# Fused cross-attention and expert layer: P times V for two quads of heads in one group, four buffers for P, and the output normalised ahead of a maximum

## What is computed

```python
qh = (q @ Wq + bq).reshape(B, LQ, HEADS, D_K).transpose(0, 2, 1, 3)
kh = (k @ Wk + bk).reshape(B, LKV, HEADS, D_K).transpose(0, 2, 1, 3)
vh = (v @ Wv + bv).reshape(B, LKV, HEADS, D_K).transpose(0, 2, 1, 3)
scores = jnp.einsum('bhqd,bhkd->bhqk', qh, kh) * scale
attn = jax.nn.softmax(scores, axis=-1)
out = jnp.einsum('bhqk,bhkd->bhqd', attn, vh)
concat = out.transpose(0, 2, 1, 3).reshape(B, LQ, D_MODEL)
return concat @ Wo + bo
```

## Time and profile before

| what | before |
|---|---|
| median of three runs | 1063.61 us (1063.42 to 1067.46) |
| profiled execution, its own time | 1062.17 us |
| its span | 1060.4 us |
| TensorE multiplies busy | 885.8 us, 84% |
| TensorE weight loads busy | 700.0 us, 66% |
| VectorE busy | 698.5 us, 66% |
| ScalarE busy | 616.3 us, 58% |
| GpSimd busy | 227.5 us, 21% |
| granted TensorE clock, mean | 0.928 |

### The profile page before, as it was taken

How to read it: one execution, slowest core, us unless ns; L and a number is a source line. 1 busy time by engine, 2 the same in 40 slices (tenths; PEclk the granted TensorE clock), 3 DMA queues, 4 the chain that set the end, 5 groups by cost and what they waited for, 6 DMA issues and landing times. The chain is left out here.

```text
span 1060.4 us, 23352 instructions
## 1 busy us (share of the span) xinstructions
PE 885.8 (84%) x8843; PEld 700.0 (66%) x8843; DVE 698.5 (66%) x1884; ACT 616.3 (58%) x1305; POOL 227.5 (21%) x192
## 2 busy tenths in 40 slices
PE   0763789999999999999999850039999999999995
PEld 0331357767676776777676640029999999999995
DVE  6681267787778777877878648857566576574540
ACT  1432477777777777777776531009568476485671
POOL 1343000000000000000000004042556466565313
PEclk9986699999999999999999975559999999999998
DMA  2211674565566456546644012031533524525203
GB/s 69 70 35 35 154 161 116 143 156 124 118 156 143 122 131 157 129 121 147 151 114 101 24 34 77 0 127 34 125 83 95 128 46 123 128 49 137 40 11 35
DMA packets 96209, 104.63 MB, mean 99 GB/s; under 512 B 11744, under 2 KB 92272, under 8 KB 96112
## 3 DMA queue, kind: packets, MB, share of 16 engines
q1 hardware_dynamic: 84128, 88.50, 33.5%
q0 software_dynamic: 10752, 14.69, 8.1%
q10 hardware_dynamic: 1232, 0.12, 0.1%
HBM read 39.60 MB, written 14.68 MB: 51 GB/s over the span
## 5 line engine op out<-in xcount | busy, mean ns | idle before, releaser
L405 DVE TENSOR_REDUCE a_nm<-a_pS 112x1 f32<-112x375 f32 x512 | 264.7, 543 | 122.8 <-PE a_pS L500 119.8
L350 ACT ACTIVATE a_P<-a_pT 128x448 f32<-128x448 f32 x384 | 209.2, 546 | 136.0 <-PE a_pT L494 135.3
L500 PE MATMUL a_pS<-kst,a_qst 96*112 96x375 bf16 x512 | 151.9, 336 | 3.6 <-DVE a_nm L405 3.1
L494 PE MATMUL a_pT<-a_qst,kst 98*128 98x112 bf16 x1536 | 139.3, 213 | 1.6 <-DMA a_qst<-a_mT 1.5
L494 PEld LDWEIGHTS a_pT<-a_qst,kst 98*128 98x128 bf16 x1536 | 107.4, 99 | 42.7 <-issue 8.6
L1278 PE MATMUL e_p<-w2h,e_hh 128*128 128x256 f32 x448 | 128.3, 286 | 0.0
L1278 PE MATMUL e_p<-w2h,e_hl 128*128 128x256 f32 x448 | 126.2, 282 | 0.0
L1278 PE MATMUL e_p<-w2l,e_hh 128*128 128x256 f32 x448 | 126.2, 282 | 0.0
L358 ACT ACTIVATE kp<-a_pK,bk 128x375 bf16<-128x375 f32 x192 | 109.5, 570 | 19.1 <-PE a_pK L524 12.1
L1133 POOL DMA_INDIRECT out_dram<-e_y,e_idx x56 | 88.3, 1577 | 134.0 <-ACT e_y L1162 130.3
L879 POOL MEMSET r_factors<- 128x1 f32 x15 | 0.6, 98 | 540.2 <-POOLq L236 539.9
(11 more groups left out here) (193 smaller groups left out, 1506.3 us busy)
## 6 DMA issues: line engine op xcount, KB each, us to landing
kst<-kp SPq DMA_DIRECT2D x192, 192.0 KB, 3.6
w<-in_L_ffn_W_dram SPq DMA_DIRECT2D x16, 1024.0 KB, 7.5
a_qst<-qp SPq DMA_DIRECT2D x96, 112.0 KB, 3.8
a_craw<-in_ctx_dram SPq DMA_DIRECT2D x32, 128.0 KB
q_xin<-in_x_dram SPq DMA_DIRECT2D x8, 448.0 KB, 3.8
a_xb<-in_x_dram SPq DMA_DIRECT2D x32, 112.0 KB, 3.2
out_dram<-a_x SPq DMA_DIRECT2D x32, 112.0 KB, 2.5
xn_scratch<-a_x SPq DMA_DIRECT2D x32, 112.0 KB, 2.6
```

What stands on the lines that cost most here:

```text
L350: act.activation(P[quad % 2][:, c, :], pT[u % 2][:, 0:4 * LQ], ACT.Exp).then_inc(exp_done, 1)
L405: dve.tensor_reduce(nm[:, h:h + 1], pS[h % 2][0:LQ, 0:LK], AXX, ALU.max, negate=True).then_inc(s_used, 1)
L494: last = pe.matmul(pT[u % 2][:, j * LQ:(j + 1) * LQ], kst[b % 4][:, h, c * 128:(c + 1) * 128], q_of(b, slice(None), h), start=True, stop=True)
L500: pe.matmul(pS[h % 2][0:LQ, 0:LK], q_of(b, slice(0, ROWS), h), kst[b % 4][0:ROWS, h, 0:LK], start=True, stop=True).then_inc(s_ready, 1)
```

## The change

`P` gets four buffers, one for each quad. Quads 0 and 1 of element m + 1 are multiplied in step 7 of round m, one behind the other, and quads 2 and 3 in step 1 of the next round. VectorE does `normalise(m)` first in step 4, before the maximum of head 14 and the two instructions of the layer norm.

```diff
-        P = [sb(f"P{i}", [128, 3, 4 * LQ]) for i in range(2)]
+        P = [sb(f"P{i}", [128, 3, 4 * LQ]) for i in range(4)]
...
-                act.activation(P[quad % 2][:, c, :], pT[u % 2][:, 0:4 * LQ], ACT.Exp).then_inc(exp_done, 1)
+                act.activation(P[quad][:, c, :], pT[u % 2][:, 0:4 * LQ], ACT.Exp).then_inc(exp_done, 1)
...
                 for u in range(12):
+                    if u == 4 and live(m):
+                        normalise(m)
                     b = m + 2 if u < 6 else m + 3
...
-                    if u == 4 and live(m):
-                        normalise(m)
                     if u == 9 and live(m):
                         residual(m)
...
-                                         P[quad % 2][0:n, c, j * LQ:(j + 1) * LQ], start=(c == 0), stop=(c == 2),
+                                         P[quad][0:n, c, j * LQ:(j + 1) * LQ], start=(c == 0), stop=(c == 2),
...
                     if u == 1 and live(m):
+                        weighted(m, 2)
                         weighted(m, 3)
-                    if u in (4, 7, 10) and live(m + 1):
-                        weighted(m + 1, (u - 4) // 3)
+                    if u == 7 and live(m + 1):
+                        weighted(m + 1, 0)
+                        weighted(m + 1, 1)
```

## The result

The changed kernel takes 1070.27 us (median of 9 runs, 1069.04 to 1074.89) against 1063.42 us for the kernel before (9 runs beside them). The ratio is 1.0066, 95% interval 1.0045 to 1.0087: slower by 0.7%, forecast 1069.2 us.

The account below looks back on a forecast made before the run. TensorE's order sets the pace, at its edge behind VectorE. 0.13 us slower in 27 rounds (3.5), plus 1.5 and 0.6, gives 5.6 us on 1062.17: 1067.8, with 1.44 for the median 1069.2 us; range 1059 to 1084.

Parts of the forecast that it names:

- Step 9 to step 2: Round's stretch where quad 2's W leaves step 10 and step 1 gains a second W: 0.24 us slower.
- Step 2 to step 9: Round's stretch where quad 0's W leaves step 4, normalise goes first and step 7 gains a W: 0.11 us faster.
- nothing on VectorE holds TensorE back: Rival for the whole round: both pairs save and the cc wait ends, 27 us, 1042 us median; chance 0.10.
- The debt of the moved normalise: Rival at heads 14 to 2: normalise's 0.63 us on VectorE delays TensorE in full, 14 us more, 1083 us; chance 0.15.
- gate in part: Rival: VectorE starts its run sooner at step 9, second W nearer 0.55 us, 1058.5 to 1064.5 us; chance 0.09.
- The rule on draining: TensorE's entries into W: changing tiling mode drains TensorE, so by this rule alone halving the entries is a clean gain.
- the three rounds after the last keys: Rounds without K to give 0.36 us back: 3 x 0.49 = 1.5 us slower.
- no term below comes from the clock: Slices holding attention show a granted clock of 9, full speed at 2.4 GHz, so the clock adds nothing.
- The last round with its added W: Last round, where nothing else fills TensorE: the added W costs 0.6 us.

Follow-up runs that it names:

- e3: Changed kernel with the residual's three VectorE instructions spread behind the maxima of steps 9, 10 and 11: 15.17 us a round, 1058.65 us.
- e4: e2 with four buffers and quads 2 and 3 together in step 1, quads 0 and 1 still alone: 15.01 us a round, 1053.76 us.
- e2: Kernel before with only normalise moved first in step 4, W one quad at a time, two buffers: 14.76 us a round, 1047.07 us.
- e10: Kernel before with normalise first, residual spread, last key cut ahead of the exponential, quads 2 and 3 together: 1028.72 us, against 1030.53 without that pair.
- e5: Kernel before with four buffers for P and nothing else: 15.40 us a round, 1062.72 us, ratio 1.0005.
- e11: Changed kernel run and profiled again without any edit (the second trace): 15.48 us a round, 1069.47 us, ratio 1.0068 to the kernel before.

## Why the prediction was right

**Step 9 to step 2** was put at 0.24 us slower. It measured 314.14 - 308.17 = 5.97 against 307.42 - 301.70 = 5.72: 0.25. S of head 8 stayed (3.38 us behind T of step 9), the wait came, and K gave back 0.33 where 0.36 was said, with T of step 11 0.71 us sooner and not 0.8 (309.81 - 308.17 against 304.05 - 301.70): T of step 1 comes after 312.39 - 308.17 = 4.22 against 306.25 - 301.70 = 4.55. e3 and e4 show the cause and the price alone.

**Step 2 to step 9** was put at 0.11 faster and measured 0.17 (9.51 against 9.68). L566 came the 0.72 sooner and head 15 cost its 0.1. The difference is small terms: the second W costs 0.58, not 0.60 (1.30 us for the pair in step 1, 307.42 - 306.70 = 0.72 for the single one in the trace before), and L588 takes 1.02 in place of 1.09 behind it. Hence 0.09 a round in place of 0.13, 2.4 us in place of 3.5.

**The rivals.** That nothing on VectorE holds TensorE back is refuted at its own point of decision: 3.38 us from T of step 9 to S of head 8. The price of this rival was added up wrongly: 1063.6 - 27 is 1036.6 us, not 1042; both lie in its range. The debt of the moved normalise was not paid in full; e2 alone, 0.63 us a round faster, shows that it costs little. VectorE did not gate in part either: its run starts 308.73 - 308.17 = 0.56 us behind T of step 9, and did so 302.27 - 301.70 = 0.57 us behind it.

**The rule on draining.** Halving the mode switches did save work: a single W was put at 0.81 us and the second of a pair costs 0.58. Of the 0.81 only 0.71 came free (1.01 - 0.30 us, from S to K in step 10), because K there now waits for ScalarE, which the prediction did not see. The Trainium skill's rule (TensorEngine Tiling (Array Packing), Key Properties) speaks of TensorE alone, and in e10, where both other waits are removed, the 0.2 us still went to this one and to the first K.

**The mis-sized term** is "the three rounds after the last keys", put at 3 x 0.49 = 1.5 us. They cost 4.4 in the first trace: by about what was forecast, and by stretches at half clock, which I had excluded with "no term below comes from the clock". A price for one such stretch: the kernel before has it in its third round, 14.57 us, and e5, the same order without it, takes 13.10, so 1.5 us; the second round of the changed kernel gives 16.23 - 14.63 = 1.6, with it and without. Three stretches against one are 2 x 1.5 = 3.0 us, and 1.4 is left, near the 1.5 of the forecast; but the one round without a stretch in both kernels, the second of e11, costs 0.31 us more than before and not 0.49. The stretch in the kernel before was there to be seen; a slice of the page is 26.5 us and showed a 9.

The last round with its added W was put at 0.6 and measured 25.1 - 23.9 = 1.2 in the first trace and 26.4 - 23.9 = 2.5 in the second. Here too the clock may be the rest: in this part it was at half level for 8.5 us before, for 10.0 in the first trace and for 13.0 in the second, which has a stretch of 3.4 us more (from 626.9). As an estimate, time at half level costs at most half of itself: 0.7 and 2.2 us more than before, beside the 0.6. No run shows this alone.

The first trace adds up to 2.4 + 4.4 + 1.2 = 8.0 us, the medians differ by 6.85, and the forecast was 5.6: one term 1.1 too large, the two others 3.5 too small. That the forecast of the median is right within 1.1 us is therefore in part luck. The course of the round was foreseen, the clock was not, and it differs between executions of the same kernel: those of the changed kernel run from 1065.98 to 1075.05 us.

## What to carry to other kernels

A saving on the busiest engine counts only up to the next semaphore that another engine sets in its own fixed order: walk both timelines side by side and look for a consumer that is on time by 0.05 us, since the list of waits hardly shows it. Independent work between a producer and the wait for its consumer is not overhead, it is cover: W in steps 4 and 10 hid the normalise and the residual, and grouping it laid both bare. Measure the halves of an edit apart: here one half was worth 1.6%, the other cost 2.3 points, and only their sum was to be seen.

## What the hardware showed that I had not expected

TensorE's clock fell to its half level for 3.4 us in the middle of a stage in which it had been busy 13.62 of 15 us. In the changed kernel it did so in the rounds that had lost their key products, the first time behind the wait of 0.66 us at head 8, and never in the 27 rounds before, which have the same wait and more work around it. The Trainium skill, TensorE: Matmul & The Clock Gate, section "HAM oscillation — how this bites in real kernels", tells of a kernel whose clock falls again at each wait between two groups of multiplies; the waits there are for DMA and several times longer than those here. This case's traces agree that the clock can fall again inside a running stage, at 1.5 us a time, and in the changed kernel they show it behind waits of no more than 0.9 us; that such a wait is enough they do not show, since the second round of e11 has one of 0.66 us and the third of e5 two of 0.61 and 0.88 us, and neither has a fall.

A multiply that starts after a wait takes longer in the trace, and its weight load then starts together with it and not ahead of it: 0.04 us more for S (0.37 against 0.33) and 0.10 us for the fp32 pair of K (0.90 against 0.80, again in e3). So many short waits cost more than their sum.
